# Flamingo layer on one core: token sums of the first group on VectorE, two down products emptied later, norms of the tail in two parts, banks of attention in the order of release

## What is computed

```
x = x + tanh(g_xattn) * xattn(layernorm(x), ctx, ctx)
x = x + tanh(g_ffn) * ffn(layernorm(x))
```

```
base   = y @ W_org.T
q      = mean of y over the tokens @ Wq.T
coeffs = softmax(q @ lora_keys.T / sqrt(K))        # 8 experts
h      = y @ lora_down[e]                          # 8 x 64 columns
delta  = sum over e of coeffs[e] * (h[e] @ lora_up[e])
ffn    = base + delta
```

## Time and profile before

| | us |
|---|---|
| median of 3 runs | 1475.55 (1474.72 to 1478.16) |
| profiled execution, its own time | 1479.68 |
| its span in the trace | 1477.9 |
| TensorE busy | 1412.9 (96%) |
| VectorE busy | 671.0 (45%) |
| ScalarE busy | 397.4 (27%) |
| GpSimd busy | 234.7 (16%) |
| mean granted clock of TensorE | 0.973 |

### The profile page before, as it was taken

One profiled execution on the slowest core, in us unless ns is written; L12 is line 12 of the kernel. 1 busy time (PEld: TensorE's weight loads), 2 busy tenths in 40 slices (PEclk: granted clock), 3 DMA queues, 4 the chain that ended last, 5 costly groups with the idle time before them and its releaser, 6 DMA issues.

```text
span 1477.9 us, 22384 instructions
## 1 busy us (share of the span) xinstructions
PE 1412.9 (96%) x8656; PEld 1163.0 (79%) x8656; DVE 671.0 (45%) x1371; ACT 397.4 (27%) x736; POOL 234.7 (16%) x400
## 2 busy tenths in 40 slices
PE   7999999999999999769999999999889999999998
PEld 6887887878888888657777777878788878878787
DVE  5322121221655545456776766776737334234210
ACT  3311101101212212234555454554333020021100
POOL 0000000000000000014555555555500000000000
PEclk9999999999999999868999999999979999999999
DMA  6753644546457677966777767776532211202101
GB/s 202 205 165 129 149 150 128 143 135 146 160 166 188 167 186 184 257 202 183 234 218 216 224 201 211 214 207 186 186 143 82 90 39 63 94 20 78 52 29 57
DMA packets 181720, 224.87 MB, mean 152 GB/s; under 512 B 24048, under 2 KB 122352, under 8 KB 181616
## 3 DMA queue, kind: packets, MB, share of 16 engines
q1 hardware_dynamic: 166160, 189.11, 44.2%
q10 hardware_dynamic: 15456, 34.35, 7.3%
HBM read 136.89 MB, written 85.46 MB: 150 GB/s over the span
## 4 chain that ended last, share of the span: by engine, by line
PE 79%; DMA 11%; DVE 4%; SPq 3%; issue 2%; ACT 1%; ACTq 0%; DVEq 0%
PE bank L156 19%; PE bank L158 19%; PE bank L157 19%; DMA early_q<-q_rows 6%; PE bank L901 4%; DMA q_in<-q_rows 3%; PE bank L866 3%; PE bank L290 3%; PE bank L886 2%; PE bank L324 2%; PE bank L849 2%; PE bank L851 2%; PE bank L850 2%; DMA first_q<-q_rows 1%; SPq L190 1%
## 5 line engine op out<-in xcount | busy, mean ns | idle before, releaser
L1006 DVE TRANSPOSE_TENSOR_REDUCE part<-bank 128x16 f32<-128x512 f32 x256 | 167.9, 693 | 32.2 <-PE bank L866 30.4
L964 ACT ACTIVATE probT<-bank 128x512 f32<-128x512 f32 x256 | 138.8, 596 | 117.2 <-PE bank L886 117.0
L156 PE MATMUL bank<-place_a,w_hi 128*128 128x512 f32 x384 | 152.6, 397 | 7.9 <-DVE place_a L149 7.9
L510 DVE SCALAR_TENSOR_TENSOR stage_lo<-bank,bias_mixed,stage_hi 128x512 fp32r<-128x512 f32 x64 | 47.9, 748 | 233.0 <-ACT stage_hi L512 233.0
L158 PE MATMUL bank<-place_a,w_lo 128*128 128x512 f32 x384 | 151.0, 393 | 0.0
L157 PE MATMUL bank<-place_a,w_hi 128*128 128x512 f32 x384 | 150.7, 392 | 0.0
L512 ACT ACTIVATE stage_hi<-bank,bias_mixed 128x512 fp32r<-128x512 f32 x64 | 44.1, 689 | 265.3 <-PE bank L158 250.0
L849 PE MATMUL bank<-place_a,oT_hi 128*128 128x512 f32 x256 | 108.9, 425 | 3.6 <-ACT gated L928 3.6
L1343 DVE SCALAR_TENSOR_TENSOR raw_d<-bank,gates,raw_d 128x512 f32<-128x512 f32 x32 | 24.0, 750 | 179.9 <-PE bank L158 179.9
L156 PE MATMUL bank<-place_a,yT_hi 128*128 128x512 f32 x256 | 102.5, 400 | 0.0
L156 PE MATMUL bank<-place_b,place_a 128*128 128x512 f32 x256 | 100.4, 392 | 1.4 <-DVE place_c L149 1.4
(11 more groups left out here) (195 smaller groups left out, 2723.4 us busy)
## 6 DMA issues: line engine op xcount, KB each, us to landing
k_rows<-stage_hi SPq DMA_DIRECT2D x128, 128.0 KB, 2.4
v_pad<-v_out SPq DMA_DIRECT2D x32, 512.0 KB, 2.7
v_place<-v_pad ACTq DMA_DIRECT2D x32, 512.0 KB, 4.9
q_rows<-stage_hi SPq DMA_DIRECT2D x124, 128.0 KB, 2.4
early_q<-q_rows SPq DMA_DIRECT2D x128, 100.0 KB
q_in<-q_rows SPq DMA_DIRECT2D x84, 100.0 KB
early_k<-k_rows SPq DMA_DIRECT2D x42, 196.0 KB
k_in<-k_rows SPq DMA_DIRECT2D x42, 196.0 KB
```

The costliest lines, as they stand in the source:

```text
L156: nc.tensor.matmul(bank_ap, sh, mh, start=(i == 0), stop=False)
L510: lambda bank: nc.vector.scalar_tensor_tensor(out=lo[:], in0=bank[:], scalar=bias, in1=hi[:].bitcast(F32), op0=ALU.add, op1=ALU.subtract),
L964: act.activation(probT[o % NPT][:, i].rearrange("k a p q -> k (a p q)"), two_bank[i][:], ACT.Exp).then_inc(s_exp, 1)
L1006: dve.tensor_reduce(part[o % NS][:, :, 2 * i:2 * i + 2, :].rearrange("k a p b -> k a (p b)"), one_bank[i][:].rearrange("k (a b t) -> k a b ...
```

## The change

Four things.

1. `turn` begins with the bank that projection releases first (`len(jobs)` instead of `len(jobs) - 2`).
2. Norms of the tail: the statistics in slot `start`, inverse and normalise in `start + 2`, root still in `start + 1`; the starts become +0, +4, +6, +8 (before +1, +3, +5, +9) from `OCTS + LAG`.
3. `first_sums` is no longer a TensorE job: after the transposes of all four batches, eight jobs without TensorE or ScalarE part reduce the eight transposed banks on VectorE, as the later groups do.
4. The first two down products are filled before their coefficients exist, as jobs whose emptying is a `passed` step (VectorE sets one element of a tile `idle` and counts the job as done). The scores stand between the two, and each is really emptied by a later job that comes to the same bank (`stage`), behind the spread. The W_org splits are spread over the new order, the lora_up splits stand behind the last down product, and the norm and transposes of the first batch of group 1 move behind the first half and the second half of the first output.

```diff
-            else:
+            elif job.dve:
                 self.wait_filled(dve, n + 1)
             if job.dve_wait:
                 job.dve_wait(dve)
-            job.dve(self.bank(n)).then_inc(self.emptied, 1)
+            if job.dve:
+                job.dve(self.bank(n)).then_inc(self.emptied, 1)
+            else:
+                job.passed(dve).then_inc(self.emptied, 1)
...
-            turn = [(len(project_line.jobs) - 2 + i) % len(banks) for i in range(len(banks))]
+            turn = [(len(project_line.jobs) + i) % len(banks) for i in range(len(banks))]
...
-            NORMS = list(zip(FIRST_ORDER, (OCTS + LAG + 1, OCTS + LAG + 3, OCTS + LAG + 5, OCTS + LAG + 9)))
+            NORMS = list(zip(FIRST_ORDER, (OCTS + LAG, OCTS + LAG + 4, OCTS + LAG + 6, OCTS + LAG + 8)))
...
                     for n, (i, start) in enumerate(NORMS):
-                        if start <= s < start + 2:
+                        if s in (start, start + 2):
                             stages = norm.vector_stages(n, first_y[i], lambda dve: dve.wait_ge(s_first[i], 16))
-                            for stage in stages[2 * (s - start):2 * (s - start) + 2]:
+                            for stage in stages[s - start:s - start + 2]:
                                 stage(dve)
...
-            def first_sums():
...
-                def pe_fn(bank):
-                    for k in range(KC):
-                        for i in range(GB):
-                            last = nc.tensor.matmul(bank[:, k * GB + i:k * GB + i + 1], first_y[i][:, k * P:(k + 1) * P],
-                                                    ones[:], start=True, stop=True, skip_group_check=True)
-                    return last
-                return line.add(Job(pe_fn, lambda bank: nc.vector.tensor_copy(msum[:].rearrange("p k b -> p (k b)"),
-                                                                              bank[:, 0:KC * GB]), pe_wait=ready))
+            def first_sums(b, half):
+
+                part = slice(4 * half, 4 * half + 4)
+                return line.add(Job(None, lambda bank: nc.vector.tensor_reduce(
+                    msum[:, part, b:b + 1], bank[:].rearrange("p (q s) -> p q s", q=4), AX.X, ALU.add)))
...
                 def landed(eng):
                     eng.wait_ge(s_up[k], 16)
+
+                def free(act):
+                    act.wait_ge(line.emptied, ring.last[4 + k])
+                    landed(act)
...
                     act=lambda bank: nc.scalar.activation(up_hi[:, k, :], up_raw[k], ACT.Copy),
-                    act_wait=landed, dve_wait=landed))
+                    act_wait=free, dve_wait=landed))
...
-            def h_job(g, c, coef_end):
+            def h_job(g, c, coef_end, stage=None):
...
-                return line.add(Job(pe_fn, lo_fn, act=hi_fn, reads=group_end(g),
-                                    act_wait=lambda act: act.wait_ge(line.emptied, coef_end)))
+                def coefs(act):
+                    act.wait_ge(line.emptied, coef_end)
+
+                if stage == "products":
+                    return line.add(Job(pe_fn, None, reads=group_end(g), passed=lambda dve: dve.memset(idle[:], 0.0)))
+                if stage is not None:
+                    def products(act):
+                        coefs(act)
+                        line.wait_filled(act, stage)
+                    assert (len(line.jobs) + 1 - stage) % len(banks) == 0
+                    return line.add(Job(None, lo_fn, act=hi_fn, act_wait=products))
+                return line.add(Job(pe_fn, lo_fn, act=hi_fn, reads=group_end(g), act_wait=coefs))
...
-            sums_end = first_sums()
-            y_jobs(0)
+            for n in range(GB):
+                y_jobs(n)
+            for n in range(GB):
+                for half in range(2):
+                    sums_end = first_sums(n, half)
+            h0_end = h_job(0, 0, None, "products")
             scores_end = first_scores()
-            y_jobs(1)
+            h1_end = h_job(0, 1, None, "products")
+            coefs_end = first_coefs()
 
             def first_exponentials(act):
                 act.wait_ge(line.emptied, scores_end)
                 exponentials(act)
             line.jobs[-1].act_pre = first_exponentials
-            y_jobs(2)
-            score_end = first_coefs()
-            y_jobs(3)
...
             base_chunks(2)
+            coef_end = spread_job(coefs_end)
+            base_chunks(1)
+            h_job(0, 0, coef_end, h0_end)
+            base_chunks(1)
+            h_job(0, 1, coef_end, h1_end)
+            base_chunks(3)
+            h_job(0, 2, coef_end)
+            base_end = base_chunks(1)
+            h_job(0, 3, coef_end)
+            for k in range(LC):
+                h_end = up_chunk(k)
             for g in range(NG):
-                for c in range(LC):
-                    h_end = h_job(g, c, coef_end)
-                    if c < LC - 1 or g:
+                if g:
+                    for c in range(LC):
+                        h_end = h_job(g, c, coef_end)
                         carrier = line.jobs[-1]
-                    if g == 0:
-                        if c < 2:
-                            base_end = base_chunks(3)
-                        else:
-                            for k in ((0, 1, 2), (3,))[c - 2]:
-                                h_end = up_chunk(k)
                 for i in range(GB):
                     n, more = g * GB + i, g + 1 < NG
-                    if more:
+                    if more and n:
 
                         y_norm(n + GB, carrier)
                         y_jobs(n + GB)
                     carrier = out_job(n, 0, h_end)
                     if more and i == GB - 1:
                         score_end = score_job(g + 1)
+                    if n == 0:
+                        y_norm(GB, carrier)
+                        carrier = out_job(n, 1, h_end)
+                        y_jobs(GB)
+                        continue
```

## The result

| | before | changed |
|---|---|---|
| median of 6 runs, us | 1475.45 (1471.20 to 1478.16) | 1465.32 (1464.57 to 1468.58) |
| ratio | | 0.9938 (95% interval 0.9921 to 0.9956) |
| profiled execution, us | 1479.68 | 1468.58 |
| its span, us | 1477.9 | 1465.4 |
| mean granted clock | 0.973 | 0.980 |

The change makes the kernel faster, by 10.1 us of the median (0.7%). The ratio of the table is one of means and gives 9.1 us, with an interval of 6.5 to 11.7. The forecast was 1460.2, 15.3 us less. The measured median lies just inside its range of 1456.0 to 1466.0, and the time that the ratio gives, 0.9938 of 1475.45 or 1466.3, just outside. The direction and most of the mechanism were right. A third of the gain is missing, and the question of the experiments is where it went.

What follows compares the result with a forecast made beforehand. TensorE, busy nearly all the time, was taken as the bound. Its terms put the second output pair at 1123.5 instead of 1138.80, 15.3 us earlier: 1475.55 becomes 1460.2, forecast 1458.5 to 1462 (0.58), wider range 1456.0 to 1466.0.

Steps and rivals of the forecast that it cites:

- Tail: Tail of attention: gate gap 0.3 instead of 3.6 us, keys start at 1065.4, 4.6 us before the 1069.96 of now.
- End of attention: Norms and last gates: norm 3 ends at 1069.7 (now 1072.9), ScalarE free for splits at 1071.3 after the last store.
- Sums: Column sums: 13.2 us leave TensorE; the first down product needs only VectorE's first sum and starts at 1077.7.
- The first product: 7.25: First down product takes 7.25 us as now, 1.65 more than the others because of a half-clock spell.
- Rival (a): First down product: low clock for longer, all 24 matmuls at 0.43, 4.8 instead of 1.65 us, so 1463.4; chance 0.12.
- hidden: Coefficients between scores and spread: some 3 us alone, covered by the second product's 5.6; cover gone would cost 2.75.
- The third product: 5.6: Third down product, behind the spread: 5.6 us, half of the 11.2 us for the last two products.
- up_lo: 1.4: First output: TensorE waits 1.4 us for the up splits, which all stand behind the last down product.
- (b): Tail of attention does not shorten, norms end at 1072.9 as now, everything behind shifts by 3.3, so 1463.5; chance 0.12.
- (c): More than forecast: full clock at the first product or shorter store hold, 1.7 to 3 us more, 1457.9; chance 0.09.
- (d): Half clock stays on through down products and first output pair: 1478 at 96 matmuls, 1492 at all; chance 0.02.
- (e): First down product waits for all eight sums, 4.2 us come back, 1464.4; chance 0.04 together with other small losses.

Runs made afterwards that it cites:

- norms_undone: The changed kernel with the norms of the tail put back as before; median 1468.49 us, ratio 0.9950 to the kernel before.
- spread_early_b: The changed kernel with the spread's copy ahead of the W_org splits and later W_org splits moved so the third product reuses the spread's bank; 1464.87 us, ratio 0.9922.
- spread_early: The changed kernel with the copy of the spread ahead of the W_org splits on VectorE; median 1468.87 us, ratio 0.9957 to the kernel before.
- coefs_first: The changed kernel with the coefficients job one place earlier, ahead of the second down product; median 1462.76 us, ratio 0.9910 to the kernel before.
- turn_undone: The changed kernel with the bank order of attention as before; median 1464.87 us, ratio 0.9930 to the kernel before.
- up_early: The changed kernel with the splits of two up chunks ahead of the last down product's split; median 1462.98 us, ratio 0.9912 to the kernel before.
- all3: The changed kernel with coefficients ahead of the second product, last x_mid stores behind the high splits, two up splits earlier; 1457.96 us, ratio 0.9881 to the kernel before.
- products_early_undone: The changed kernel with no down product ahead of its coefficients, sums still on VectorE; median 1468.73 us, ratio 0.9949 to the kernel before.
- late_stores: The changed kernel with the last two stores of x_mid issued by ScalarE behind its high splits; median 1466.08 us, ratio 0.9920 to the kernel before.

## Why the prediction was right, and where it was wrong

In the steps of the prediction, with 1.67 us added to times of the changed kernel's profile, so that both count from the same end of attention:

- *Banks: 0.* Right, and for the reason given: VectorE makes `stage_lo` itself.
- *Tail.* Right. TensorE has no gap at the gate and 0.37 us at the fourth half (forecast 0.3 and 0.4). The keys start at 1063.97 + 1.67 = 1065.64 (forecast 1065.4). The norm's normalise beside a GpSimd add took 1.75 us, and the add 1.75 instead of 1.30, so it did hold up the add before gate (14,1) by 0.45 us, and the kernel had room for that. The shorter gap at the gate is on no path to the first product (norms_undone); the sum rightly went over the norms.
- *End of attention.* Norm 3 ended at 1068.13 + 1.67 = 1069.80 (forecast 1069.7), the last gate started at 1069.03 (1068.9), the lo splits ended at 1076.98 (1076.9). The 2.4 us that held ScalarE had the right size, but only 0.33 us of them are the last issue; the rest is mostly its wait for the last gate and GpSimd's last add.
- *Sums.* First product at 1077.63 (forecast 1077.7), behind 4.96 us of waiting (some 4: the transposes ended earlier). The chain through VectorE was right to 0.1 us over 31.5.
- *The first product: 7.25.* It and the scores took 8.36 instead of 7.75, 0.6 more. Rival (a), low clock for longer, came in part: 9 half-clock matmuls of 24, and 5 to 13 over the twelve profiles.
- ***"hidden"*: the step that failed.** The forecast let the coefficients run beside the second product, "some 3 us alone, beside the 5.6", and took 1.35 us from that product's end to the third. It took 3.57. I had asked how long the coefficients' own work is and not when VectorE may start it; the order of the jobs with the rule of `wait_filled` answered that ahead of any run. I had named the price of this cover missing, 2.75 us, which is near the 2.2 that came.
- *The third product: 5.6.* It took 7.24. I took the half clock for a matter of the long wait before the first product; the short waits around the spread brought a second spell. With the step above this is 3.9 of the 4.6 us that the rest of the way lost against the forecast, and the first product has 0.6 of it.
- *up_lo: 1.4.* The wait is there, 1.33 by the trace and 1.6 by the distance. The forecast cost it well, but not as a thing to mend.
- *Rivals.* (b), (c), (d) and (e) did not happen: the tail shortened, the clock was back within nine matmuls, and the product started with the first sum while the others ran to 1081.75.
- *Sign of being wrong: another time of attention.* From its first `part` matmul to the fixed point attention took 430.07 us before and 428.49 in the changed kernel, but 424.93 to 432.26 over the twelve profiles. That sign tells nothing, since the profiles differ by more on their own.

The median fell by 10.1 us, the way by 10.8. I had carried the way's 15.3 us to the median one for one, and that step held as far as the interval of 6.5 to 11.7 us can tell.

## What to carry to other kernels

Work counts as hidden only when you know what lets its first instruction start. In a list of jobs with counting semaphores that is everything ahead of it in the list, not only what it reads: the coefficients, a job of VectorE alone, stood behind a product and so waited for it. The same for a ring of banks: what stands eight places ahead must be emptied, whether it used the bank or not.

Price a removed stretch together with the wait that takes its place: 13.2 us of TensorE work were worth 5.0 alone, and 7.3 more lay in giving TensorE something to do in the meantime.

## What the runs showed of the hardware

- A wait of 0.95 us with eight 4x4 matmuls behind it, between two full down products, was followed by seven or more matmuls at 1.2 GHz, 1.6 us lost, in every run that had it (spread_early_b with 7, though the next wait was only 0.27). Up to four matmuls of the third product still started 0.2 us apart before the clock fell (four in norms_undone, none in spread_early). The prediction had no low clock there.
- The number of half-clock matmuls in the first product varies between profiles in which all that stands ahead of it is the same: 9 (changed), 7 (coefs_first and turn_undone), 8 (up_early), 6 (spread_early_b), each behind 4.95 us of waiting. At 0.2 us each that is a spread of 0.6 us in the way. In spread_early, with the same order of work but half-clock transposes and 3.29 us of waiting, it was 5. The Trainium skill ("TensorE: Matmul & The Clock Gate", What's actually happening) says that the number is run-variable, and gives 6, 11 and 14 for one kernel; the trace agrees in kind. What brought 13 in all3 and products_early_undone stays open.
- The transposes ahead of the first product ran at full clock in most profiles and at half in that of late_stores (2.67 us for 16, not 1.91) and spread_early (3.16). They cost nothing in the second, where ScalarE came later anyway, and part of the gain in the first.
- The wait for `up_lo` cost more than its idle time in the trace: 1.33 us of idle, 1.6 us from the fourth product to the second pair.
- Whether matmuls kept up during the 4.96 us wait would save the half clock of the first product was not tried: all eight banks are held there by transposes that ScalarE and VectorE read.
